# Statistics sums shared between VectorE and TensorE, and one-hots in fp8 with block sums added by VectorE, in a four-layer graph network

## The chip, the cores and the metric

The kernel runs on one core of one Trainium2 chip. The metric is the device time of one execution in microseconds (us); lower is better. TensorE is written PE, VectorE DVE, ScalarE ACT, GpSimd POOL and SyncE SP, as in the profile.

## What is computed

6250 nodes with 64 features each and 200000 edges (source, destination, 32 edge features) go through four residual layers. Cut to the parts that the change touches:

```python
z = concatenate([h[src], h[dst], e], axis=1)
gate = sigmoid(bn(z @ W_int + b_int)); upd = softplus(bn(z @ W_upd + b_upd))   # bn: mean and variance over all edges
agg = segment_sum(gate * upd, dst)                                            # layer 0
...
for l in range(3):                                                            # layer 2
    mask = clip(sigmoid(att(x[src], x[dst])) * 1.5 - 0.45, 0, 1)
    rowsum = segment_sum(mask, src) + 1e-6
    d = clip(rowsum ** -0.5, 0, 10)
    x = segment_sum((mask * d[src] * d[dst])[:, None] * x[dst], src)
    out = out + x
```

Layer 1 is a mean over neighbours and layer 3 an MLP message sum by destination.

## The kernel before, in words

The nodes stand in 49 blocks of 128. A first part of the program (count, place) sorts the edges twice, by the block of the source and by the block of the destination, into 288 steps of 7 tiles of 128 edges; all edges of one step belong to one block. Gathers from and sums into a block are then matmuls with one-hot matrices: for each tile a 128x128 matrix with a 1 where edge and node of the block meet. One-hots of the source order lie in DRAM as `hot_s`, their transposes as `turned_s`; `hot_d` and `turned_d` are those of the destination order. Before, `hot_s` and `hot_d` are bf16 (224 KB a step) and the turned ones fp8 (112 KB a step). `table_s` and `table_d` name the block of every step; the helper `Blocks.of` (L115 on) reads four of its entries into registers of the engine that asks, at the first of four steps, and `block_of` makes the address of a block from such a register.

Each stage is written by hand as one loop for each engine, with semaphores between them; a wait holds its engine's whole instruction stream, in order. The stages come one after the other, with a barrier between them. `each4` and `each12` unroll a loop by 4 or 12 steps, for buffers that are 4 or 12 deep. These stages are touched:

- `stage_conv_spread` (cs, 288 steps). DVE makes the one-hots by source (L1176) and splits the edge features; PE turns both (L1253, L1255) and forms the products (L1268 to L1271) into `cs_u_ps`; ACT casts and copies the turned ones (L1213, L1219, L1220) and a part of the result. SP stores `hot_s`, `turned_s` and `e_turned` and loads `cs_rec` (L1134) four steps ahead; POOL scatters the rows.
- `stage_conv_stats` (ct, 288 steps). DVE does four things with 896 columns in each step: the one-hot by destination of step it + 2 (L1339), the value v (L1354), the sum of the squares of the step before (L1346), and the sum of v (L1360). ACT squares v (L1386), and stages and casts the rest. PE turns the one-hot (L1402) and multiplies (L1414). SP stores `hot_d` and `turned_d`, and loads `ct_u` for step it + 4 (L1308), once ACT has squared step it.
- `stage_masks` (mask, once for each of three layers, 288 steps in 72 quads of 4). PE makes a row part for each step (L2014), ACT copies it into `mask_cols` (L1968), POOL adds the gathered columns onto it by an indirect DMA (L1956), and DVE multiplies by the attention vector (L2047) and reduces (L2052). After the fourth step of a quad, DVE `weigh`s the quad before: five instructions on 28 columns and more (L2037 to L2039, then `split3` at L806 to L809), each of which waits for the one before it. Then PE `collect`s (L2002): 28 matmuls of 3 columns that add the mask by one-hot into one PSUM bank `mask_sums_ps` for all 49 blocks, at an address from `Blocks`. SP loads `turned_s` and `hot_s` a quad at a time. At the end the bank is copied to `rowsum` (L2058).
- `stage_hop` (hop, three times, 288 steps). POOL gathers `hop_x` (L2104); ACT weights six of the seven tiles (L2120) and DVE the seventh (L2134); DVE splits them into three bf16 parts (L2143, then L2149); PE adds them by one-hot into seven PSUM banks `hop_sums_ps` for all blocks (L2167), at an address from `Blocks`. SP loads the one-hots by source, 12 steps ahead (L2085). At the end `add_zeros` closes the banks and DVE copies 3136 columns (L2153).

`stage_conv_messages` (cm) isn't changed, but it already does what the change brings to others: its sums go to two small PSUM areas, and DVE adds each to its block of `acc` (L1615), with `Blocks` on DVE:

```python
def collect(it, i, s):
    blocks = table.of(it, i)
    dve.wait_ge(summed, it + 3)
    dve.wait_ge(added, it + 2)
    s.wait()
    dve.sem_inc(gate, 1)
    to = block_of(acc, blocks[0])
    nc.vector.tensor_tensor(to, to, sums[i % 2][:, 0, :], ALU.add).then_inc(added, 1)
```

## Time and profile before

| what | value |
|---|---|
| runs | 12580.16 us median of 3 (12571.6 to 12588.71) |
| profiled execution | 12564.72 us, its span 12563.0 us |
| busy, share of the span | PE 63%, PE weight loads 59%, DVE 65%, ACT 55%, POOL 41% |
| mean granted clock of PE | 0.779 |
| cs | 2459 to 3438 us |
| ct | 3467 to 4625 us |
| mask, three times | 6869 to 7468, 8550 to 9151, 10230 to 10829 us |
| hop, three times | 7757 to 8215, 9438 to 9896, 11117 to 11577 us |

The time of the profiled execution lies 1.7 us above its span. An instruction's duration runs from its start to its end; instructions of one engine overlap, so the distance of two starts says what one costs the engine when nothing is waited for. "Idle before" is time in which the engine did nothing ahead of an instruction, and behind the arrow stands what ended it. "DVEq" and "SPq" are the sequencers of DVE and SP: register loads and the issue of DMAs.

### The profile page before, as it was taken

To read this page: it belongs to the slowest core of one execution; us is meant where nothing else is said; L and a number is where in the kernel's file an instruction comes from. 1 tells how busy PE (TensorE), PEld (TensorE's weight loads), DVE (VectorE), ACT (ScalarE), POOL (GpSimd) and SP (SyncE) were. 2 spreads that over 40 slices of the span, in tenths; PEclk is the share of its full clock that TensorE was granted. 3 is DMA by queue.
4 is the path that set the end of the run, shared out by engine and by line. 5 is a ranking of instruction groups with operands and counts; after the bars stand their busy time and mean duration, and the time that the engine had idled before them with its cause. 6 is when DMAs were issued, how large, how long until landed. Compare 5 with 4: busy or idle time off the path is not lost. (4 is left out here: it accounts for less than half of the span.)

```text
span 12563.0 us, 438885 instructions
## 1 busy us (share of the span) xinstructions
PE 7912.2 (63%) x149095; PEld 7405.0 (59%) x149106; DVE 8207.7 (65%) x17786; ACT 6913.4 (55%) x17614; POOL 5175.5 (41%) x4482
## 2 busy tenths in 40 slices
PE   6444444488855549995766656666666666565765
PEld 6333333488745448885656656565665566565765
DVE  6777777588799999981750762925718527358047
ACT  1222222299855559986217448965479764587530
POOL 2777777444300001110630752706707338345044
PEclk8555555599978879998979669787697787787997
DMA  5555543299967759987949999979999799997997
GB/s 205 166 171 167 169 140 84 83 348 348 326 195 202 201 173 319 323 275 264 346 127 349 288 262 354 297 263 300 284 324 316 226 329 290 290 335 231 366 361 226
DMA packets 1430365, 3241.49 MB, mean 258 GB/s; under 512 B 392074, under 2 KB 973252, under 8 KB 1419042
## 3 DMA queue, kind: packets, MB, share of 16 engines
q1 hardware_dynamic: 1054798, 2289.98, 52.1%
q0 software_dynamic: 331264, 823.09, 24.7%
q10 hardware_dynamic: 44116, 125.96, 3.3%
q8 instruction: 113, 1.85, 0.1%
q14 instruction: 74, 0.61, 0.0%
HBM read 2042.53 MB, written 1129.76 MB: 253 GB/s over the span
## 5 line engine op out<-in xcount | busy, mean ns | idle before, releaser
L1956 POOL DMA_INDIRECT mask_cols<-cols_all,mask_index x864 | 1372.1, 1588 | 1339.1 <-ACT mask_index L1965 1172.0
L521 POOL DMA_INDIRECT rows_s<-place_rec,place_index x1568 | 1631.1, 1040 | 538.1 <-issue 528.7
L596 PE MATMUL place_slot_ps<-place_runs,place_oh_turned 50*128 50x100 f32 x3136 | 725.8, 423 | 1231.6 <-DVE place_runs L635 1213.6
L2104 POOL DMA_INDIRECT hop_x<-cols_all,hop_index x864 | 981.2, 1136 | 1237.4 <-ACT hop_index L2111 920.0
L596 PEld LDWEIGHTS place_slot_ps<-place_runs,place_oh_turned 50*128 50x128 f32 x3136 | 683.0, 327 | 1265.9 <-issue 1265.6
L2120 ACT ACTIVATE hop_parts<-hop_x,mask 128x64 f32<-128x64 f32 x5184 | 1265.4, 334 | 47.6 <-DMA hop_x<-cols_all,hop_index 28.1
L2047 DVE SCALAR_TENSOR_TENSOR mask_hidden<-mask_cols,att 128x448 f32<-128x448 f32 x864 | 538.5, 623 | 1085.5 <-DMA mask_cols<-cols_all,mask_index 1028.8
L2167 PE MATMUL hop_sums_ps<-hop_parts,hop_onehot 128*128 128x64 bf16 x18144 | 876.0, 216 | 472.3 <-DVE hop_parts L2149 398.2
L2167 PEld LDWEIGHTS hop_sums_ps<-hop_parts,hop_onehot 128*128 128x128 bf16 x18144 | 777.0, 113 | 573.6 <-issue 572.7
L1478 POOL DMA_DIRECT2D cm_onehot<-hot_d x288 | 152.1, 528 | 2031.1 <-POOLq L104 1229.9
L2014 PE MATMUL mask_part_ps<-mask_now,mask_turned 128*128 128x64 bf16 x18144 | 912.5, 231 | 37.4 <-issue 20.9
L1968 ACT COPY mask_cols<-mask_part_ps 128x448 f32<-128x448 f32 x864 | 460.5, 533 | 841.2 <-PE mask_part_ps L2014 829.9
L550 ACT COPY place_pair_now<-place_pair 128x8 f32 x196 | 38.7, 197 | 1599.0 <-issue 1585.6
L2014 PEld LDWEIGHTS mask_part_ps<-mask_now,mask_turned 128*128 128x128 fp8e4 x18144 | 888.9, 124 | 42.9 <-issue 42.7
L2134 DVE TENSOR_TENSOR hop_parts<-hop_x,mask 128x64 f32<-128x64 f32 x864 | 189.6, 219 | 863.7 <-DMA hop_x<-cols_all,hop_index 845.0
L1687 PE MATMUL hop_in_rows_ps<-hop_in_now,hop_in_turned 128*128 128x64 bf16 x18144 | 571.7, 194 | 279.9 <-DMA hop_in_turned<-turned_d 134.0
L1687 PE MATMUL att_in_rows_ps<-att_in_now,att_in_turned 128*128 128x64 bf16 x18144 | 574.0, 194 | 253.3 <-DMA att_in_turned<-turned_d 115.6
L1687 PEld LDWEIGHTS hop_in_rows_ps<-hop_in_now,hop_in_turned 128*128 128x128 fp8e4 x18144 | 552.5, 99 | 299.4 <-issue 299.3
L1687 PEld LDWEIGHTS att_in_rows_ps<-att_in_now,att_in_turned 128*128 128x128 fp8e4 x18144 | 555.1, 99 | 272.5 <-issue 272.5
L1159 POOL DMA_INDIRECT rows_all<-cs_u,cs_index x288 | 393.9, 1368 | 639.1 <-DVE cs_u L1196 637.8
L2052 DVE TENSOR_REDUCE mask_logit<-mask_hidden 128x7 f32<-128x448 f32 x864 | 536.1, 621 | 131.2 <-DVE mask_hidden L2047 11.7
L2002 PE MATMUL mask_sums_ps<-mask_mask,mask_onehot 128*128 128x3 bf16 x6048 | 192.2, 166 | 669.5 <-DVE mask_mask L809 358.6
(392 smaller groups left out, 26453.3 us busy)
## 6 DMA issues: line engine op xcount, KB each, us to landing
cols_all<-att_in_rows SPq DMA_DIRECT2D x216, 896.0 KB
mask_onehot<-hot_s SPq DMA_DIRECT2D x216, 896.0 KB
cols_all<-hop_in_rows SPq DMA_DIRECT2D x216, 896.0 KB
hop_onehot<-hot_s SPq DMA_DIRECT2D x864, 224.0 KB
rows_all<-blank SPq DMA_DIRECT2D x72, 1808.0 KB
ct_u<-rows_all SPq DMA_DIRECT2D x288, 452.0 KB
cm_v<-rows_all SPq DMA_DIRECT2D x288, 448.0 KB
cm_onehot<-hot_d POOLq DMA_DIRECT2D x288, 448.0 KB
```

The costliest lines, as they stand in the source:

```text
L521: nc.gpsimd.indirect_dma_start(m.rows_s.rearrange("p n w -> (p n) w"), bass.IndirectOffsetOnAxis(index[:, j, t:t + 1], 0), rec[:, j, t, :] ...
L596: last = nc.tensor.matmul(slot_ps[b][:, t, 0:2 * NBK], oh_turned[:, b, t, :], runs[:, b, t, :], start=True, stop=True)
L1159: nc.gpsimd.indirect_dma_start(rows_d, bass.IndirectOffsetOnAxis(index[:, i, :], 0), u[:, i, :], None).then_inc(scattered[i], 16)
L1687: last = nc.tensor.matmul(rows_ps[i][:, t, :], turned[:, s, i, t, :], now[:, i, n, :], start=n == 0, stop=n == 2)
L1956: nc.gpsimd.indirect_dma_start(cols[:, n, :], None, table, bass.IndirectOffsetOnAxis(index[:, n, :], 0), compute_op=ALU.add).then_inc(arri ...
L1968: nc.scalar.copy(cols[:, n, :], part_ps[n % 4].rearrange("p c f -> p (c f)")).then_inc(laid, 1)
L2014: last = nc.tensor.matmul(part_ps[i][:, t, :], turned[:, s, i, t, :], now[:, i, n, :], start=n == 0, stop=n == 2)
L2047: nc.vector.scalar_tensor_tensor(out=hidden[:, j, :, :], in0=cols[:, s * 4 + i, :].rearrange("p (c f) -> p c f", f=F), scalar=0.0, in1=b2( ...
L2052: nc.vector.tensor_reduce(logit[:, s, i * BATCH:(i + 1) * BATCH], hidden[:, j, :, :], AX.X, ALU.add).then_inc(logits, 1)
L2104: nc.gpsimd.indirect_dma_start(x[:, n, :, :].rearrange("p c f -> p (c f)"), None, table, bass.IndirectOffsetOnAxis(index[:, n:n + 1], 0)). ...
L2120: last = nc.scalar.activation(parts[:, i, 0, t * F:(t + 1) * F], x[:, s * 4 + i, t, :], ACT.Copy, scale=mask[:, bass.ds(it * BATCH + t, 1)])
L2167: last = nc.tensor.matmul(block_of(sums, blocks[0]), onehot[:, s, i, t, :], upper(parts[:, i, q, t * F:(t + 1) * F]), start=False, stop=False)
```

## The change

There are two parts. In ct the sum of v is divided: DVE adds four of the seven tiles (512 columns), and PE adds the other three (384 columns) with one f32 matmul of the identity a step into a PSUM bank that is copied out at the end. For source-ordered one-hots, cs makes them in fp8, `hot_s` in DRAM is half as wide, and mask and hop load them so; in both of these stages each block sum goes to a small PSUM area of its own, and DVE adds it to its block in SBUF. PE no longer reads the block table there; DVE does.

```diff
 def stage_conv_spread
-        onehot = sb("onehot", [P, 4, BATCH, P], bf16)
+        onehot = sb("onehot", [P, 4, BATCH, P], fp8)
...
-                                            ALU.is_equal).then_inc(hot, 1)
+                                            ALU.is_equal, saturate=False).then_inc(hot, 1)
 def stage_conv_stats
+        totaled = sem("totaled")
+        OWN = 4
+        total_ps = ctx.enter_context(nc.psum_tensor("ct_total_ps", [P, 512], fp32))[:, 0:(BATCH - OWN) * W].rearrange("p (c w) -> p c w", w=W)
...
                     dve.wait_ge(squared, it + 1)
+                    dve.wait_ge(totaled, it + 1)
...
-                    nc.vector.tensor_tensor(sum_acc[:], sum_acc[:], v[:, i % 2, :, :], ALU.add).then_inc(summed, 1)
+                    nc.vector.tensor_tensor(sum_acc[:, 0:OWN, :], sum_acc[:, 0:OWN, :], v[:, i % 2, 0:OWN, :], ALU.add).then_inc(summed, 1)
...
+                dve.wait_ge(totaled, IT + 3)
+                nc.vector.tensor_copy(sum_acc[:, OWN:BATCH, :], total_ps)
...
                     last.then_inc(spread, 1)
+                    if not isinstance(it, int) or it > 0:
+                        add_up(it - 1, (i - 1) % 2)
+
+                def add_up(it, j):
+                    pe.wait_ge(valued, it + 3)
+                    pe.sem_inc(gate, 1)
+                    nc.tensor.matmul(total_ps.rearrange("p c w -> p (c w)"), m.ident[:], v[:, j, OWN:BATCH, :].rearrange("p c w -> p (c w)"),
+                                     start=False, stop=False).then_inc(totaled, 1)
 def stage_masks
-        onehot = sb("onehot", [P, 3, 4, BATCH, P], bf16)
+        onehot = sb("onehot", [P, 3, 4, BATCH, P], fp8)
...
-        sums = ctx.enter_context(nc.psum_tensor(f"{name}_sums_ps", [P, 512], fp32))[:, 0:3 * NB].rearrange("p (b c) -> p b c", c=3)
+        sums = [ctx.enter_context(nc.psum_tensor(f"{name}_sums_ps{j}", [P, 512], fp32))[:, 0:12].rearrange("p (h c) -> p h c", c=3)
+                for j in range(3)]
+        added = sem("added")
...
                     pe.wait_ge(masked, quad + 1)
+                    pe.wait_ge(added, quad * 4 + 4)
                     pe.sem_inc(gate, 1)
                     for h in range(4):
-                        blocks = quads.of(quad * 4 + h, h)
                         for t in range(BATCH):
-                            last = nc.tensor.matmul(block_of(sums, blocks[0]), onehot[:, s, h, t, :], mask3[:, s, h * BATCH + t, :],
-                                                    start=False, stop=False)
+                            last = nc.tensor.matmul(sums[s][:, h, :], onehot[:, s, h, t, :], mask3[:, s, h * BATCH + t, :],
+                                                    start=t == 0, stop=t == BATCH - 1)
...
+                def add_rows(quad, s):
+                    dve.wait_ge(summed, quad + 1)
+                    for h in range(4):
+                        blocks = quads.of(quad * 4 + h, h)
+                        dve.wait_ge(added, quad * 4 + 12 + h)
+                        dve.sem_inc(gate, 1)
+                        to = block_of(rowsum, blocks[0])
+                        nc.vector.tensor_tensor(to, to, sums[s][:, h, :], ALU.add).then_inc(added, 1)
...
                         weigh(k * 3 + s - 1, (s - 1) % 3, k, order)
+                    if i == 3 and (not isinstance(it, int) or it > 18):
+                        add_rows(k * 3 + s - 4, (s - 1) % 3)
...
-                dve.wait_ge(summed, QUADS + 1)
-                nc.vector.tensor_copy(rowsum, sums)
+                for quad in range(QUADS - 4, QUADS):
+                    add_rows(quad, quad % 3)
 def stage_hop
-        onehot = sb("onehot", [P, 3, 4, BATCH, P], bf16)
+        onehot = sb("onehot", [P, 3, 4, BATCH, P], fp8)
...
-        sums = ctx.enter_context(nc.psum_tensor(f"{name}_sums_ps", [P, 56, F], fp32))
+        sums = [ctx.enter_context(nc.psum_tensor(f"{name}_sums_ps{j}", [P, 512], fp32))[:, 0:F] for j in range(4)]
+        added = sem("added")
...
                     nc.vector.tensor_tensor(last, rest, upper(rest), ALU.subtract).then_inc(parted, 1)
+                    if not isinstance(it, int) or it > 1:
+                        collect(it - 2, (i - 2) % 4)
+
+                def collect(it, i):
+                    blocks = table_s.of(it, i)
+                    dve.wait_ge(summed, it + 5)
+                    dve.wait_ge(added, it + 4)
+                    dve.sem_inc(gate, 1)
+                    to = block_of(acc, blocks[0])
+                    nc.vector.tensor_tensor(to, to, sums[i], ALU.add).then_inc(added, 1)
+                nc.vector.memset(acc, 0.0).then_inc(added, 1)
...
-                dve.wait_ge(summed, IT + 5)
-                nc.vector.tensor_copy(acc, sums[:, 0:NB, :])
...
-                    blocks = blocks_s.of(it, i)
+                    pe.wait_ge(added, it + 1)
...
-                add_zeros(nc, m, sums[:], False).then_inc(summed, 1)
 def build
-        m.hot_s, m.hot_d = (dram(n, [P, NBT, C * P // 2]) for n in ("hot_s", "hot_d"))
+        m.hot_s, m.hot_d = dram("hot_s", [P, NBT, C * P // 4]), dram("hot_d", [P, NBT, C * P // 2])
```

## Rows read from the trace of the kernel before

**Rows 1.** Windows, one a stage (cs, ct, first mask, first hop): stretch, length, busy time by engine, clock, DMA share, GB/s.

```profile
2459.00:3438.00 979.00, 838.09 (x14112) 796.54 (x14112) 806.35 (x2304) 872.66 (x1440) 393.92 (x288) 0.99 0.97 343
3467.00:4625.00 1158.00, 630.62 (x8065) 577.16 (x8065) 1153.88 (x1153) 645.62 (x1148) 0.00 (x0) 0.81 0.72 200
...
6869.00:7468.00 599.00, 366.63 (x8066) 355.70 (x8066) 442.32 (x1081) 274.25 (x938) 456.33 (x288) 0.67 1.06 276
...
7757.00:8215.00 458.00, 293.23 (x6060) 257.02 (x6062) 403.33 (x866) 422.88 (x1800) 327.40 (x288) 0.76 0.92 289
```

**Rows 2.** Timeline of ct: start, duration, engine, line, operation.

```profile
4001.20 1.21 DVE L1354 TENSOR_TENSOR ct_v<-ct_v_ps,ct_u 128x896 f32<-128x896 f32 x1
...
4003.84 0.35 SPq L1308 DMA_DIRECT2D ct_u<-rows_all  x1
...
4004.20 1.21 DVE L1339 TENSOR_TENSOR ct_onehot<-iota_p,ct_u 128x896 bf16<-128x896 f32 x1
```

**Rows 3.** Timeline of DVE in cm.

```profile
5001.38 0.39 DVE L1615 TENSOR_TENSOR acc<-acc,cm_sums_ps 128x64 f32 x1
5001.51 1.26 DVE L1591 TENSOR_TENSOR cm_v<-cm_v_ps,cm_v 128x896 f32<-128x896 f32 x1
```

**Rows 4.** Groups by line, PE: busy, mean ns | idle before, releasers.

```profile
L1402 PE MATMUL ct_turn_ps<-ident_b,ct_onehot 128*128 128x128 bf16 x2016 | 186.9, 242 | 553.2 <-DVE ct_onehot L1339 553.2
...
L940 PE MATMUL att_hid<-turned_l,w_att 65*128 65x448 f32 x84 | 44.7, 671 | 5.5 <-PEq L104 5.5
```

**Rows 5.** Timeline at the start of ct.

```profile
3462.37 1.78 SPq L1308 DMA_DIRECT2D ct_u<-rows_all  x4
...
3466.27 3.32 DVE L1339 TENSOR_TENSOR ct_onehot<-iota_p,ct_u 128x896 bf16<-128x896 f32 x3 [0.49 <-DMA ct_u<-rows_all]
```

**Rows 6.** Groups by line, ACT in cs.

```profile
L1213 ACT COPY cs_e<-cs_rec 128x448 f32<-128x448 f32 x288 | 162.7, 565 | 73.7 <-PE cs_e_ps L1255 37.8 <-DMA cs_rec<-rows_s 30.3
```

**Rows 7.** DMA of the mask stage, 6900 to 7400 us: SP's queue, packets, MB, share.

```profile
q1 hardware_dynamic: 17854, 85.34, 43.7%
```

**Rows 8.** Timeline of DVE in the first mask stage, around two quads' ends.

```profile
7107.64 0.21 DVE L809 TENSOR_TENSOR mask_mask<-mask_mask_now,mask_mask 128x28 bf16<-128x28 f32 x1
7108.36 0.63 DVE L2047 SCALAR_TENSOR_TENSOR mask_hidden<-mask_cols,att 128x448 f32<-128x448 f32 x1 [0.51 <-issue]
...
7113.37 0.62 DVE L2047 SCALAR_TENSOR_TENSOR mask_hidden<-mask_cols,att 128x448 f32<-128x448 f32 x1
...
7114.67 0.17 DVE L2037 TENSOR_SCALAR mask_mask_now<-mask_logit 128x28 f32<-128x28 f32 x1
7114.87 0.18 DVE L2038 TENSOR_SCALAR mask_mask_now<-mask_mask_now 128x28 f32<-128x28 f32 x1
7115.21 0.20 DVE L2039 COPY mask<-mask_mask_now 128x28 f32 x1 [0.16 <-DVE mask_mask_now L2038]
7115.30 0.19 DVE L806 CAST mask_mask<-mask_mask_now 128x28 bf16<-128x28 f32 x1
...
7116.19 0.62 DVE L2047 SCALAR_TENSOR_TENSOR mask_hidden<-mask_cols,att 128x448 f32<-128x448 f32 x1
```

**Rows 9.** One line's instructions, L2047 in the first mask stage: durations, first and last start.

```profile
L2047 DVE SCALAR_TENSOR_TENSOR mask_hidden<-mask_cols,att x288: 614/625/667, 6885.2 to 7461.0; 128x448 f32<-128x448 f32 x144
```

**Rows 10.** Waits in the first mask stage, 6900 to 7440 us: total, times, longest.

```profile
DVE mask_hidden L2047 <- DMA mask_cols<-cols_all,mask_index: 46.7, 89, 1.5
```

**Rows 11.** One line's instructions (L121, L1615) in cm: duration ns min/median/max.

```profile
L121 DVEq TENSOR_LOAD <-table_d x72: 340/344/607, 4708.3 to 5619.6; - x72
...
L1615 DVE TENSOR_TENSOR acc<-acc,cm_sums_ps x288: 214/386/417, 4710.2 to 5630.6; 128x64 f32 x144
```

**Rows 12.** Timeline of DVE in the first hop stage.

```profile
7902.17 0.63 DVE L2143 TENSOR_TENSOR hop_parts<-hop_parts 128x448 f32<-128x448 f32 x1
...
7902.94 0.62 DVE L2149 TENSOR_TENSOR hop_parts<-hop_parts 128x448 f32<-128x448 f32 x1
7903.60 0.62 DVE L2143 TENSOR_TENSOR hop_parts<-hop_parts 128x448 f32<-128x448 f32 x1
```

More of the change, by code:

```diff
@@ L1991, in _ @@
             def _(pe):
-                quads = Blocks(nc, pe, m.table_s)
-                add_zeros(nc, m, sums, True)
                 def collect(quad, s, k):
@@ L2028, in _ @@
                 dve.sem_inc(logits, 2)
+                dve.sem_inc(added, 11)
+                quads = Blocks(nc, dve, m.table_s)
+                nc.vector.memset(rowsum, 0.0).then_inc(added, 1)
+                def add_rows(quad, s):
[6 more added lines that the diff above has]
+                        nc.vector.tensor_tensor(to, to, sums[s][:, h, :], ALU.add).then_inc(added, 1)
                 def weigh(quad, s, k, order):
@@ L2149, in step @@
                     nc.vector.tensor_tensor(last, rest, upper(rest), ALU.subtract).then_inc(parted, 1)
+                    if not isinstance(it, int) or it > 1:
[7 more added lines that the diff above has]
+                    nc.vector.tensor_tensor(to, to, sums[i], ALU.add).then_inc(added, 1)
+                table_s = Blocks(nc, dve, m.table_s)
+                dve.sem_inc(added, 3)
+                nc.vector.memset(acc, 0.0).then_inc(added, 1)
                 scale_seventh(0, 0, 0)
-                each12(dve, step)
-                dve.wait_ge(summed, IT + 5)
-                nc.vector.tensor_copy(acc, sums[:, 0:NB, :])
+                each12(dve, step, first=2)
+                collect(IT - 2, (IT - 2) % 4)
+                collect(IT - 1, (IT - 1) % 4)
             @block.tensor
             def _(pe):
-                blocks_s = Blocks(nc, pe, m.table_s)
-                add_zeros(nc, m, sums[:], True)
                 def step(it, s, i, k, more, _):
@@ L2166, in step @@
                         for q in range(3):
-                            last = nc.tensor.matmul(block_of(sums, blocks[0]), onehot[:, s, i, t, :],
-                                                    upper(parts[:, i, q, t * F:(t + 1) * F]), start=False, stop=False)
+                            last = nc.tensor.matmul(sums[i], onehot[:, s, i, t, :],
+                                                    upper(parts[:, i, q, t * F:(t + 1) * F]),
+                                                    start=t == 0 and q == 0, stop=t == BATCH - 1 and q == 2)
                     last.then_inc(summed, 1)
                 each12(pe, step)
-                add_zeros(nc, m, sums[:], False).then_inc(summed, 1)
 def build(nc, a, out):
```

7 lines of the change are left out of this document (5 added, 2 removed).

## The prediction, written before the changed kernel ran

> **What bounds the kernel now.** The stages follow one another, so the change is priced stage by stage, and the first view is that of the windows [rows 1]. In ct DVE is busy 1154 of 1158 us: nothing else sets that time. In cs no engine is full (PE 838, ACT 873 of 979 us), while the DMA engines are busy 0.97 of it. In mask no engine is full either (DVE 442, POOL 456 of 599 us) and the DMA share is 1.06, so the DMAs seem to bound it; but a busy share hides short waits between dependent instructions, so the timeline must say how much room DVE has. In hop ACT leads with 423 of 458 us, DVE with 403 is close behind, DMA 0.92.
>
> **Statistics (ct).** DVE starts an 896-column instruction each 1.00 us: from L1354 at 4001.20 to L1339 at 4004.20 are three [rows 2], so a step is 4.00 us. In cm a sum of 64 columns takes 0.13 between starts [rows 3]; so a column costs (1.00 - 0.13) / 832 = 1.05 ns, and 512 columns 0.60 us. DVE alone would go at 3.60: 288 x 0.40 = 115 us less. PE gets an f32 matmul of 384 columns; 448 columns took 671 ns [rows 4], so about 0.6 us and a weight load. PE waits 553 us / 288 = 1.92 us a step for the one-hot just there [rows 4], so that is hidden; without this cover it would be 288 x 0.6 = 170 us. What is late next is the load of `ct_u`. It is issued 2.64 us after the start of v (4003.84 against 4001.20 [rows 2]), since SP waits for the square, and serves the one-hot of step it + 4, which DVE starts 1.00 us before v of step it + 4 - 2, two steps on. The first load of the stage took 3.90 us from its issue to the start of the one-hot, which waited for it [rows 5]. So with a step of P, 2P - 1.00 is at least 2.64 + 3.90, and P at least 3.77 us. At 4.00 there are 0.46 us to spare over the two steps, and no wait; at 3.60 there would be. I take 3.78: 288 x 0.22 = **-63 us**; bounds 0 (the load gets slower as it is asked for more often) and -115 (later loads faster than the first).
>
> By the Trainium skill (DMA: Bandwidth & Descriptors, Anatomy of one DMA) a DMA costs about 2.0 us fixed and its bytes / 436e3: for 452 KB about 3.1 us, an estimate by that page, under which ct would give the whole -115. The 3.90 us of [rows 5] speak against it.
>
> **One-hots in fp8, cs.** DVE, PE and ACT issue what they did. SP's store of `hot_s` falls from 224 to 112 KB a step: 33 MB of 343 GB/s x 979 us = 336 MB [rows 1], a tenth. If the DMAs alone bound cs that would be 98 us. But ACT is at 873 of 979, and only part of its idle time ends with a DMA: 30 us at L1213 [rows 6]. I take these and a third more for the like on DVE: **-40 us**; bounds 0 and -98.
>
> **Masks.** Removed: half the one-hot load. 60 quads in 500 us by 896 KB are 55 of the 85 MB of SP's queue with its share of 0.437 [rows 7]; half of that is 0.14 of DMA time. Also removed: PE's table reads, its closing zero matmul and the copy of `rowsum`, all small beside the rest. Added on DVE for each quad: `add_rows`. What is DVE's room? A step without waits is L2047 to L2037, 7113.37 to 7114.67 = 1.30 us; `weigh` is 7114.67 to 7116.19 = 1.52; where the loop branches, one quad in three, the way from L809 to L2047 is 0.72 (7107.64 to 7108.36); I take 0.5 of it as extra [rows 8]. A quad is 4 x 1.30 + 1.52 + 0.17 = 6.89 us, 72 quads 496. DVE's part of the stage goes from 6885.2 [rows 9] to the end at 7468 [rows 1], 583 us, so it waits about 87; 46.7 us of 540 stand as waits for the gathers [rows 10]. DVE is thus 85% filled by dependent work and not, as the busy time says, 74%.
>
> The price of `add_rows`: first the table is read into registers, 0.344 us [rows 11]; with the register work, the wait and the address I take 0.83 from the last instruction of `weigh` to the first add. Then each of the three further adds waits for the one before it, by `added`, and takes its address from a register. Its nearest row is L2038 to L2039: 0.34 us between starts, 0.18 of it duration and 0.16 wait and address [rows 8]; the mark on `gate` is an instruction of its own here, for which I add 0.1. So 0.44 each. The way back to L2047 costs 0.1. Sum 0.83 + 3 x 0.44 + 0.1 = 2.25 us a quad, 162 a stage. Bounds: 1.1 (four adds at 0.20, the table read not much more than its 0.344) and 3.0 (each add at the 0.386 of L1615 [rows 11] and 0.26 around it). The new quad is 9.1 us; POOL's 456 us for 288 gathers are 1.58 each, with the pause of about 0.3 behind each 7.5 us a quad, and don't bind; neither do the DMAs with less to move. Of the waits some 8 us of start and 3 of end are left: 496 + 162 + 11 = 669 against 583, +86 a stage, **+258 us**. PE's `collect` now waits for `added` too, and behind it stand the row parts of the next quad; but DVE needs these two quads (18 us) later, so it costs nothing while POOL has under 9.1 us of work a quad.
>
> Here the Trainium skill speaks against my price (VectorE: DVE Perf Modes, The DRAIN you can't avoid): the next operation doesn't start before the pipeline is empty, with or without a semaphore, so a semaphore costs nothing extra. The trace disagrees: L806 follows L2039, on which it doesn't wait, after 0.09 us, and L2038 follows L2037, on which it does, after 0.20 [rows 8].
>
> **Hops.** A step is 1.43 us on DVE (7902.17 to 7903.60) [rows 12], paced by ACT. DVE's own need is 0.77 from L2143 to L2149 and 0.53 for the 448 columns of L2149 (0.66 are taken): 1.30. The add of 64 PSUM columns costs 0.13 between starts, as in cm [rows 3]: 1.43, a tie with ACT. One step in four also reads the table. In cm long instructions queued ahead cover that; here DVE's sequencer has only L2149's 0.53 us ahead of it for table, waits and address, by the 0.83 above and the wait of the next L2143 about 0.45 us too little: +0.11 a step, and branches +0.04. 288 x 0.15 = 43 us, of which I take 27 as absorbed by waits that the stage has today (458 us against 288 x 1.43 = 412), and which the halved one-hot load shrinks. The closing copy of 3136 columns (3.3 us at 1.05 ns) and the zero matmuls go, about 5 us; the memset of `acc` lies beside the first gather. Net +11 a stage, **+35 us**; bounds -60 (all open time hidden, fewer waits) and +150 (0.17 us a step more).
>
> **The sum.** -63 - 40 + 258 + 35 = +190 us, on the profiled execution's 12565 (span 12563): 12755. The median stands 15 us above that execution, and the forecast is for a median: rounded within those 15, **12760**. My forecast's own range is 12640 to 12860.
>
> **The rivals.** (1) *Waits on DVE's own work are nearly free or hidden*: `add_rows` costs 0.35 for the table and 4 x 0.2 for the adds, 1.15 us a quad, 83 a stage, which the 87 us of waits take up. Then masks +3 each, ct -63, cs -40, hops 0: about 12475, faster. It decides where the price is under 1.1 us a quad. For it: cm, where such adds cost 0.13 [rows 3]. Against: [rows 8]. 0.10. The rule of The DRAIN you can't avoid in the Trainium skill would lead here. (2) *Halved DMAs pay everywhere*: cs -90, ct -115, hops -20 each, masks as forecast: 12565 + 258 - 265 = 12558, no change. For it: DMA shares of 0.92 and more [rows 1]. Against: [rows 5, 6]. 0.10. (3) *Hops become DVE's too*: 0.17 us a step more than ACT's pace, +50 a stage: 12870. For it: the tie at 1.43 [rows 12]. 0.14. That the change doesn't do what it says gets nothing: the adds and waits are in the code.
>
> **The numbers.** Forecast 0.66, rivals 0.10, 0.10 and 0.14. The range leaves out rival 1 and part of 2: 12600 to 12890. About 0.2% (25 us) is what a measurement of this kernel can tell from no change. Faster: 0.10 and 0.03 of rival 2, 0.13; same 0.05; slower 0.82.
>
> **What would show it.** In the changed profile: ct steps of 3.78 us with DVE waiting for `ct_u` before L1339 (3.60 and no wait would be rival 2's part); masks of about 685 us with the starts of the adds 0.44 apart, and few waits for gathers left; cs near 940; hops near 470 with a gap at every fourth add. I am wrong if a mask stage stays at 600 us or under.

## The result: slower by 1.3%, by the predicted sum

The changed kernel takes **12743.42 us** (median of 4 runs, 12737.16 to 12750.6), the kernel before 12584.43 us (4 runs, 12571.6 to 12589.0): a ratio of **1.0128**, 95% interval 1.0113 to 1.0143. Predicted were 12760 us and a range of 12600 to 12890. The profiled execution took 12750.6 us with a span of 12749.0, 186 us more than the 12563.0 of the kernel before; the prediction's sum was +190.

By stage, from the first to the last instruction that writes one of the stage's own tiles, in us. The last adds of a mask stage, and the closing copy of a hop in the kernel before, write tensors that outlive the stage, and so fall into the pause behind:

| stage | before | changed | difference | predicted |
|---|---|---|---|---|
| spread (cs) | 977.8 | 934.9 | -43 | -40 |
| statistics (ct) | 1159.9 | 1109.1 | -51 | -63 |
| three masks | 597.2, 599.8, 597.4 | 671.7, 673.8, 674.2 | +225 | +258 |
| pause behind each mask | 15.9, 16.4, 15.9 | 20.1, 20.8, 20.2 | +13 | in the +258 |
| three hops | 453.5, 453.5, 455.4 | 466.3, 468.3, 465.4 | +38 | } |
| pause behind each hop | 68.5, 65.9, 72.0 | 63.5, 63.9, 67.0 | -12 | } +35 |
| placement, not touched | 2135.7 | 2142.7 | +7 | 0 |

These make +177 of the +186; the rest lies in untouched stages, no one of which moved by over 6 us. The +13 behind the masks come of the last fourteen adds, which run behind TensorE's last sum; counted to the last add, the mask stages grew by 79, 78 and 81 us. Of the -12 behind the hops some 10 are the closing copies of 3.4 us each, which are gone.

The first view is again that of the windows, one a stage, of the changed kernel (stretch and its length; then busy time of PE, PEld, DVE, ACT, POOL; TensorE's granted clock, DMA share, GB/s), to be held against [rows 1]:

```profile
2463.90:3398.80 934.90, 836.34 (x14112) 794.64 (x14112) 787.58 (x2304) 866.06 (x1440) 308.76 (x287) 0.99 0.94 323
3426.60:4535.60 1109.00, 704.37 (x8642) 533.96 (x8642) 1059.03 (x1155) 647.88 (x1152) 0.00 (x0) 0.99 0.76 210
6787.20:7458.90 671.70, 367.16 (x8064) 358.15 (x8064) 477.40 (x1359) 270.33 (x938) 450.17 (x288) 0.66 0.93 197
7754.80:8221.20 466.40, 319.57 (x6048) 286.38 (x6048) 428.43 (x1152) 430.79 (x1800) 295.74 (x288) 0.66 0.82 213
```

VectorE's busy time in the mask stage grew by 35 us only (442 to 477) while the stage grew by 75, and every engine and the DMA queues are less full than before (DMA 1.06 to 0.93). A stage that gets slower while each of its resources gets emptier waits for a chain, and only the timeline shows it. VectorE at the end of a quad of the changed kernel (start, duration, engine, line, operation, the idle time before it):

```profile
7105.73 0.21 DVE L809 TENSOR_TENSOR mask_mask<-mask_mask_now,mask_mask 128x28 bf16<-128x28 f32 x1
7106.53 0.16 DVE L2056 TENSOR_TENSOR rowsum<-rowsum,mask_sums_ps 128x3 f32 x1 [0.60 <-issue]
7106.94 0.16 DVE L2056 TENSOR_TENSOR rowsum<-rowsum,mask_sums_ps 128x3 f32 x1 [0.25 <-DVE rowsum L2056]
7107.33 0.16 DVE L2056 TENSOR_TENSOR rowsum<-rowsum,mask_sums_ps 128x3 f32 x1 [0.24 <-DVE rowsum L2056]
7107.73 0.16 DVE L2056 TENSOR_TENSOR rowsum<-rowsum,mask_sums_ps 128x3 f32 x1 [0.24 <-DVE rowsum L2056]
7108.43 0.63 DVE L2075 SCALAR_TENSOR_TENSOR mask_hidden<-mask_cols,att 128x448 f32<-128x448 f32 x1 [0.54 <-issue]
```

The first add starts 0.80 us behind L809, the others 0.41, 0.39 and 0.40 apart: four instructions with 0.64 us of work. This is a quad at whose end the loop branches: from the start of L809 to the start of the next step were 0.72 us in [rows 8], and are now 2.70, so 1.98 more. At the two ends of three where the loop doesn't branch it is 2.06 and 1.98. 72 quads at about that are some 143 us, and the waits that the stage had before take up nearly half of it.

In the statistics the step is bound by the load, as said. Timeline of two steps of the changed kernel:

```profile
4001.27 0.35 SPq L1311 DMA_DIRECT2D ct_u<-rows_all  x1
...
4002.52 1.08 DVE L1359 TENSOR_TENSOR ct_v<-ct_v_ps,ct_u 128x896 f32<-128x896 f32 x1
...
4004.40 0.86 PE L1430 MATMUL ct_total_ps<-ct_v,ident 128*128 128x384 f32 x2
4004.52 0.68 DVE L1365 TENSOR_TENSOR sum_acc<-sum_acc,ct_v 128x512 f32<-128x512 f32 x1
4005.03 0.35 SPq L1311 DMA_DIRECT2D ct_u<-rows_all  x1
4005.38 1.09 DVE L1343 TENSOR_TENSOR ct_onehot<-iota_p,ct_u 128x896 bf16<-128x896 f32 x1 [0.18 <-DMA ct_u<-rows_all]
4006.39 1.08 DVE L1359 TENSOR_TENSOR ct_v<-ct_v_ps,ct_u 128x896 f32<-128x896 f32 x1
```

The load of 4001.27 serves the one-hot of 4005.38, two steps on, which waits for it: 4.11 us from issue to use, where the first load of the stage had taken 3.90 [rows 5]. The next load is issued 2.51 us behind the start of v (4005.03 against 4002.52), 2.64 in [rows 2]. The prediction's relation with these, (2.51 + 4.11 + 1.01) / 2, gives a step of 3.82; from v to v it is 3.87 here. PE's sum of 384 columns runs as two matmuls, 0.86 us in all, beside VectorE's work, and nobody waits for it. And the clock that TensorE was granted in ct is 0.99, the 2.4 GHz level, against 0.81 [rows 1]; TensorE was busy 704 of 1109 us where it had been 631 of 1158. No time hangs on it, since VectorE waits for the load and not for TensorE.

In the hops one step in four stands out, the one with the table read:

```profile
7902.46 0.65 DVE L2180 TENSOR_TENSOR hop_parts<-hop_parts 128x448 f32<-128x448 f32 x1
7903.27 0.22 DVE L2190 TENSOR_TENSOR H<-H,hop_sums_ps 128x64 f32 x1 [0.16 <-PE hop_sums_ps L2208]
7903.44 0.62 DVE L2174 TENSOR_TENSOR hop_parts<-hop_parts 128x448 f32<-128x448 f32 x1
...
7904.22 0.62 DVE L2180 TENSOR_TENSOR hop_parts<-hop_parts 128x448 f32<-128x448 f32 x1
7904.76 0.21 DVE L2190 TENSOR_TENSOR H<-H,hop_sums_ps 128x64 f32 x1
```

From L2180 to the add are 0.81 us with the read and 0.54 without. The profile names TensorE as releaser, but this comes every fourth step.

### The profile page after: what moved, and what is told of

It is laid out like the page before. It is cut to its first block and busy times, and to the rows that moved or that the text cites. A ratio compares the mean times of both kernels' runs of the same rounds, so it can differ in the third digit from the quotient of the medians.

```text
span 12749.0 us, 445377 instructions
## 1 busy us (share of the span) xinstructions
PE 8080.8 (63%) x149631; PEld 7469.2 (59%) x149636; DVE 8275.9 (65%) x19515; ACT 6919.2 (54%) x17614; POOL 4991.2 (39%) x4482
## 5 line engine op out<-in xcount | busy, mean ns | idle before, releaser
L2135 POOL DMA_INDIRECT hop_x<-cols_all,hop_index x864 | 894.0, 1035 | 1404.2 <-ACT hop_index L2142 945.1
L2208 PE MATMUL hop_sums_ps<-hop_parts,hop_onehot 128*128 128x64 bf16 x18144 | 963.8, 224 | 453.0 <-DVE H L2190 269.9
L2208 PEld LDWEIGHTS hop_sums_ps<-hop_parts,hop_onehot 128*128 128x128 fp8e4 x18144 | 863.5, 118 | 553.2 <-issue 552.9
L2019 PEld LDWEIGHTS mask_sums_ps<-mask_mask,mask_onehot 128*128 128x128 fp8e4 x6048 | 179.3, 104 | 915.6 <-issue 915.5
L1271 PE MATMUL cs_u_ps<-cs_now,cs_turned 128*128 128x128 bf16 x6048 | 578.5, 219 | 0.0
## 6 DMA issues: line engine op xcount, KB each, us to landing
ct_u<-rows_all SPq DMA_DIRECT2D x288, 452.0 KB
```

The source lines that it names most:

```text
L1271: last = nc.tensor.matmul(at, turned[:, i, t, :], now[:, i, n, :], start=False, stop=n == 2)
L2135: nc.gpsimd.indirect_dma_start(x[:, n, :, :].rearrange("p c f -> p (c f)"), None, table, bass.IndirectOffsetOnAxis(index[:, n:n + 1], 0)). ...
L2208: last = nc.tensor.matmul(sums[i], onehot[:, s, i, t, :], upper(parts[:, i, q, t * F:(t + 1) * F]), start=t == 0 and q == 0, stop=t == BAT ...
```

## The experiments

The theory after the result had four claims: the mask loss is the serial chain of four adds at a place where VectorE has nothing else queued; the statistics' gain is cut by the ring of load, add, square, load; the hops pay for the table read; and the parts add up, since they lie in different stages. The rivals are named in the expectations. The runs came from different chips, and each group was timed beside the kernel before: a first group (12557.72 us median of the kernel before, 6 runs), a second (12553.97, 7 runs), a third on a chip on which it took 13321.95 (7 runs), and a last one (12562.89, 7 runs). Ratios are to the kernel before of the same group; stage times are to the last write of a stage tile, as above. Where an edit moves adds into or out of the pause behind a mask stage, stage and pause together are given too (613, 616 and 613 us in the kernel before, 692, 695 and 694 in the changed one).

### One part alone: the statistics

The kernel before with the changed statistics stage (its matmul onto `total_ps` with it) and nothing else.

```diff
- nc.vector.tensor_tensor(sum_acc[:], sum_acc[:], v[:, i % 2, :, :], ALU.add).then_inc(summed, 1)
+ nc.vector.tensor_tensor(sum_acc[:, 0:OWN, :], sum_acc[:, 0:OWN, :], v[:, i % 2, 0:OWN, :], ALU.add).then_inc(summed, 1)
```

> The kernel before with the statistics part alone. Theory (the parts add up, and ct is paced by the load of ct_u): ct goes from 1160 to about 1109 us as in the changed kernel, step 3.82 us, cs, masks and hops stay as before; total 50 us below the kernel before, 0.4%. Rival (in the changed kernel ct is slowed by something of the other part): ct below 1080 us here.

Measured: 12503.66 us, ratio 0.9959 (0.9939 to 0.9978). The stage takes 1103.1 us, 57 less; spread (976.7), masks (597.8, 595.1, 596.2) and hops (456.6, 456.9, 456.0) stay within 5 us of the table above. The group of the one-hots in it:

```profile
L1343 DVE TENSOR_TENSOR ct_onehot<-iota_p,ct_u 128x896 bf16<-128x896 f32 x263 | 286.8, 1090 | 35.4 <-DMA ct_u<-rows_all 27.8 <-issue 1.1
```

The wait for the load is there without any other part of the change, so the fp8 one-hots and the block sums have no share in it.

### One part alone: the block sums on VectorE, one-hots in bf16

Against the changed kernel (the statistics as before, too):

```diff
- onehot = sb("onehot", [P, 3, 4, BATCH, P], fp8)
+ onehot = sb("onehot", [P, 3, 4, BATCH, P], bf16)
```

> The kernel before with the block sums on VectorE in masks and hops alone, one-hots still bf16. Theory (VectorE's chain of add_rows paces the masks, the DMAs don't): each mask stage about 672 us, as in the changed kernel, although 112 KB a step more are loaded; cs unchanged at 978; hops 466 to 480 us, by the waits for the larger one-hots; total 240 to 290 us above the kernel before. Rival (masks are bound by the DMAs): masks above 700 us.

Measured: 12865.86 us, ratio 1.0246 (1.0216 to 1.0275). Masks 672.9, 675.5 and 680.1, hops 473.3, 474.3 and 478.0, spread 977.4. The total, 308 us over the kernel before, lies above the 240 to 290 that were expected, though each stage came as expected. The block sums alone cost the masks all that they cost in the changed kernel, and the smaller one-hots are worth at most 6 us a mask stage there. In the spread, which the sums don't touch, the 42 us from 977 to 935 come with the smaller one-hots: the two others of this group, with fp8, have 937 and 938, both with bf16 have 977 (976.7 and 977.4). The reverse, fp8 one-hots with PE's block sums as before, was not tried.

### The wait between the adds

The changed kernel with four accumulators, one for each add of a quad, summed once at the end:

```diff
- dve.wait_ge(added, quad * 4 + 12 + h)
+ if h == 0:
+     dve.wait_ge(added, quad * 4 + 12)
- to = block_of(rowsum, blocks[0])
+ to = block_of(four[:, h, :, :], blocks[0])
```

> The changed kernel with four accumulators in each mask stage, one for each of the four adds of a quad, so that an add never waits for the add before it; the four are summed once at the end of the stage (two instructions). Same number of adds. Theory (the price is the wait for VectorE's own result, 0.2 us of the 0.40 between the adds): the adds start 0.2 us apart, a mask stage falls by 72 x 3 x 0.2 = 43 us, to about 630. Rival (a wait on one's own engine costs nothing extra, the adds cost 0.4 us by themselves): masks stay at 672.

Measured: 12623.95 us, ratio 1.0052 (1.0029 to 1.0075); masks 642.1, 643.0 and 642.1, 30 to 32 less each, and about 35 less with the pauses. Its timeline at a quad's end:

```profile
7108.19 0.21 DVE L809 TENSOR_TENSOR mask_mask<-mask_mask_now,mask_mask 128x28 bf16<-128x28 f32 x1
7108.98 0.87 DVE L2058 TENSOR_TENSOR mask_four<-mask_four,mask_sums_ps 128x3 f32 x4 [0.59 <-issue]
7110.42 0.62 DVE L2077 SCALAR_TENSOR_TENSOR mask_hidden<-mask_cols,att 128x448 f32<-128x448 f32 x1 [0.57 <-issue]
```

Four adds of 0.16 us take 0.87 from the first start to the last end: (0.87 - 0.16) / 3 = 0.237 between starts, where it was 0.40. So the wait for the add before makes 0.16 us of each gap, less than the 0.2 that was expected; the rest is the add's own duration and 0.08 more. 3 x 0.16 x 72 quads are 35 us, which is what came back with the pauses. The 0.16 is the price at this place and not of every wait for an own result: in `weigh` five of the seven instructions wait so too (all but L2037 and L806), and in [rows 8] L2038 starts 0.20 behind L2037. The one at 0.34, L2039, takes an address from a register, as the adds do; whether that makes the difference no run tried. The first add still starts 0.79 behind L809: that is the table read, which this edit leaves.

### The place of the adds

The changed kernel with one add in each step, between the product and the reduction, in place of four in a row at every fourth step. Each of these adds waits for the one before it, and the table is read once a quad, as before.

```diff
+ if not isinstance(it, int) or it > 15:
+     add_row(k * 3 + s - 4, (s - 1) % 3, i)
  dve.wait_ge(hid, it + 13)
...
- if i == 3 and (not isinstance(it, int) or it > 18):
-     add_rows(k * 3 + s - 4, (s - 1) % 3)
```

> The changed kernel with the four adds of a quad put one into each step, between L2047 and the reduce that waits for it, where VectorE idles 0.24 us today. Same adds, same waits, same table read. Theory (the adds are dear only because nothing lies between them): they cost nearly nothing there but for the table read (under 0.5 us a quad); a mask stage falls to 540 to 580 us, where GpSimd's gathers (7.5 us a quad) bind. Rival (four adds cost the same wherever they stand): 672 us. Between them, about 620, the sequencer's own time counts.

Measured: **12414.44 us, ratio 0.9886 (0.9857 to 0.9915)**, faster than both kernels. Masks 568.4, 569.2 and 569.2: 104 less than in the changed kernel and 29 less than in the kernel before; with the pause behind, 24 to 26 less than before.

```profile
7106.28 0.62 DVE L2075 SCALAR_TENSOR_TENSOR mask_hidden<-mask_cols,att 128x448 f32<-128x448 f32 x1
7107.45 0.16 DVE L2056 TENSOR_TENSOR rowsum<-rowsum,mask_sums_ps 128x3 f32 x1 [0.55 <-PE mask_sums_ps L2019]
7107.67 0.62 DVE L2082 TENSOR_REDUCE mask_logit<-mask_hidden 128x7 f32<-128x448 f32 x1
7108.21 0.61 DVE L2075 SCALAR_TENSOR_TENSOR mask_hidden<-mask_cols,att 128x448 f32<-128x448 f32 x1
7108.74 0.15 DVE L2056 TENSOR_TENSOR rowsum<-rowsum,mask_sums_ps 128x3 f32 x1
7108.97 0.62 DVE L2082 TENSOR_REDUCE mask_logit<-mask_hidden 128x7 f32<-128x448 f32 x1
7109.51 0.61 DVE L2075 SCALAR_TENSOR_TENSOR mask_hidden<-mask_cols,att 128x448 f32<-128x448 f32 x1
```

Look at the step of 7108.21: with an add in it, it is 1.30 us long, exactly the 1.30 of [rows 8] without one. The reduction waits for the product in front of it anyway; the add fits into that wait, starts 0.53 behind the product, and its own wait for the add before has been over for a step. Only the step with the table read is longer, 1.93 (7106.28 to 7108.21). The profile names TensorE there, but by the code the sums that this add takes were done two quads earlier.

### What binds the masks once the adds are free

The changed kernel with the adds of the row sums and TensorE's wait for them left out.

```diff
- pe.wait_ge(added, quad * 4 + 4)
...
- if i == 3 and (not isinstance(it, int) or it > 18):
-     add_rows(k * 3 + s - 4, (s - 1) % 3)
```

> The changed kernel with the adds of the row sums in the three mask stages left out, and TensorE's wait for them with them (the row sums stay zero, so this part of the computation is missing); one-hots, block sums of TensorE and all traffic stay. In the profile of the changed kernel a mask stage takes 672 to 674 us; with one add in each step it takes 569. Theory (the adds cost only because VectorE paces the stage; without them the next limit is near 560, which is where the spread adds have come to already): 545 to 575 a stage, the kernel near 12400. Rival (the gain of the spread adds came from elsewhere and VectorE still paces the stage at 569): 500 to 540 a stage without the adds. Second rival (transfers pace the stage): not under 600.

Measured: 12409.13 us, ratio 0.9882 (0.9862 to 0.9901); masks 570.6, 571.5 and 566.5. Without any add the stages are as long as with one a step; with the pause behind, where the last adds stand, they are 2 to 7 us shorter. So spread adds cost next to nothing. The windows 6900 to 7300 us, first of this kernel, then of the one with spread adds:

```profile
6900.00:7300.00 400.00, 255.23 (x5776) 248.40 (x5774) 311.42 (x777) 195.73 (x670) 336.59 (x209) 0.68 1.05 237
```

```profile
6900.00:7300.00 400.00, 262.32 (x5891) 255.52 (x5892) 329.69 (x1002) 199.17 (x682) 335.71 (x212) 0.68 1.06 240
```

VectorE is busy 311 of 400 us without the adds and 330 with them, and the stage doesn't care: it isn't VectorE's any more. GpSimd's own row of the waits of the kernel without adds:

```profile
POOL mask_cols L1976 <- issue: 37.8, 124, 0.3
...
POOL mask_cols L1976 <- ACT mask_cols L1988: 14.6, 48, 0.3
POOL mask_cols L1976 <- ACT mask_index L1985: 11.3, 37, 0.3
```

336.6 us of gathers and 63.7 of pauses between them fill the 400. All 209 pauses are about 0.3 us, whatever the profile names as their end, so GpSimd goes from gather to gather without a longer wait. It paces the stage, at 400 / 209 = 1.91 us a gather, 7.7 a quad. In the changed kernel the same engine waited 87.5 us of the 400 for the indices, which is what an engine does that runs at another's pace, VectorE's.

### The load of the statistics

The changed kernel; SyncE's load waits for the copy of the map (L1392 there), the slot's last reader, and no longer for the square behind it:

```diff
- sp.wait_ge(squared, it + 3)
+ sp.wait_ge(mapped, it + 1)
...
- nc.scalar.copy(m.map_d[:, bass.ds(it, 1)], u[:, i, C * W + C:UW])
+ nc.scalar.copy(m.map_d[:, bass.ds(it, 1)], u[:, i, C * W + C:UW]).then_inc(mapped, 1)
```

> The changed kernel with one edit in the statistics stage: SyncE's load of the rows of step i+4 (the 452 KB that fill ct_u) waits for ScalarE's copy of the map, the last reader of that slot, and no longer for the square behind it. In the profile of the changed kernel the stage takes 1109 us in 290 steps (3.82 each) and VectorE's one-hots wait 38 us for this load. Theory (the ring of load, add, square, load paces the stage and keeps back what the removed columns gave): the load starts about 1 us earlier, the step falls to about 3.6 and the stage to 1040 to 1070, the kernel by 40 to 70 us, to about 12690. Rival (the DMA queues' own throughput, or TensorE's f32 sum of 384 columns in a step, paces it): the stage stays within 10 us of 1109.

Measured: 12662.84 us, ratio 1.0084 (1.0063 to 1.0104), against the 1.0128 of the changed kernel; the stage takes 1045.6 us, 63.5 less than in the changed kernel and 114 less than in the kernel before. The groups by line from 3500 to 4400 us:

```profile
L1344 DVE TENSOR_TENSOR ct_onehot<-iota_p,ct_u 128x896 bf16<-128x896 f32 x250 | 270.3, 1081 | 0.0
...
L1431 PE MATMUL ct_total_ps<-ct_v,ident 128*128 128x384 f32 x500 | 216.1, 514 | 0.0
```

and the window of nearly the whole stage:

```profile
3430.00:4450.00 1020.00, 685.04 (x8465) 520.23 (x8465) 1016.34 (x1128) 633.23 (x1126) 0.00 (x0) 1.00 0.81 223
```

250 steps in 900 us are 3.60 each, the step that the prediction worked out for VectorE alone. The wait for the load is gone, VectorE is busy 1016 of 1020 us, and the DMA queues carry 223 GB/s where they had carried 210. So it was the ring and not the queues.

### The table read of the hops

The changed kernel; VectorE's sequencer reads the table behind L2174, where it waits for other engines, and the add takes the values:

```diff
  nc.vector.tensor_tensor(rest, whole, upper(whole), ALU.subtract).then_inc(halved, 1)
+ if not isinstance(it, int) or it > 1:
+     table_s.of(it - 2, (i - 2) % 4)
...
- blocks = table_s.of(it, i)
+ blocks = table_s.values[i:i + 1]
```

> The changed kernel with one edit in the hops: VectorE's sequencer reads the step's block number from its table right behind the one-hots of the step, where it waits about 0.5 us for other engines anyway, and no longer between two pieces of VectorE work. Theory (in the hops the change costs VectorE's own path, the table read of about 0.34 us and the one wait more): each hop falls from 466 to 450 or so, 40 us in all, with 10 to 60 as the range. Rival (the hop is paced by the gathered rows or by TensorE, and the read lies in idle time already): each hop stays within 5 us of 466.

Measured: 12697.64 us, ratio 1.0111 (1.0091 to 1.0132), too near the 1.0128 of the changed kernel to say much by itself. The stages say more: hops 452.3, 453.0 and 452.2, 13 to 15 less each. Its timeline:

```profile
7902.66 0.62 DVE L2174 TENSOR_TENSOR hop_parts<-hop_parts 128x448 f32<-128x448 f32 x1
...
7904.10 0.62 DVE L2174 TENSOR_TENSOR hop_parts<-hop_parts 128x448 f32<-128x448 f32 x1
...
7908.44 0.61 DVE L2174 TENSOR_TENSOR hop_parts<-hop_parts 128x448 f32<-128x448 f32 x1
```

Four steps from 7902.66 to 7908.44 are 5.78 us, 1.44 or 1.45 each and none longer than its neighbours by the 0.3 us of before.

### The three edits together

Spread adds, early load and early table read in one kernel (the diffs are those above).

> The changed kernel with three edits together: in the masks one add in each step in place of four in every fourth (12414 us when it ran alone), the early load of the statistics, and the early table read of the hops. If the three gains lie in different stages and add up: 12414 - 50 (statistics) - 40 (hops) = about 12325, with 12280 to 12400 as the range. If neither the load nor the table read is on the path of its stage: 12400 to 12420.

Measured: **12310.07 us (4 runs, 12302.39 to 12316.14), ratio 0.9804 (0.9788 to 0.9821)**. Masks 569.8, 568.4 and 567.6, statistics 1045.9, hops 452.0, 450.1 and 452.4: each stage has what its edit gave alone.

### One size: four tiles on TensorE

```diff
- OWN = 4
+ OWN = 3
```

> The kernel with the three edits (12310 us) and one size changed: TensorE sums four of the seven tiles (512 columns) in the statistics, VectorE three (384). With the early load VectorE is busy 1016 of 1020 us there, so it is the bound. Theory (VectorE's step of 3.60 us loses 128 columns at about 1.1 ns each, 0.13 to 0.14 us): the stage falls from 1046 by 35 to 40 us to about 1008, the kernel to about 12272. Rival (the next limit is within that: the rows' load, a ring of 3.5 to 3.6 us, or the DMA queues at 0.81 of their time): the stage falls by under 15 us. Second rival (TensorE's f32 sum grows to be late for VectorE's next write of the same tile): the stage grows.

Measured on the slower chip: 13074.24 us, ratio 0.9818 (0.9802 to 0.9834). The statistics take 1014.5 us, 31 less than 1045.9; masks 567.9, 567.9 and 567.6. Hops are 527 to 530, not 450 to 452 as on the other chip. The ratio could not say whether the total had gained, so the kernel ran once more:

> The kernel with the three edits and four tiles on TensorE once more: its first runs came from a chip on which the kernel before took 13322 us instead of 12554, with the extra time in the stages that are paced by gathered or small transfers, and the statistics at 1014.5 us (1046 with three tiles). If that chip alone hides the gain in the total: on a chip where the kernel before takes 12550 to 12590, this takes 12270 to 12310 (12310 less 31), a ratio of 0.977 to 0.979. If the fourth tile gives the time back elsewhere: 12305 to 12340, a ratio of 0.980 or more. On a chip like the last one: 13070 to 13080 again, which tells nothing new.

Measured: **12290.12 us (4 runs, 12287.42 to 12291.0), ratio 0.9785 (0.9769 to 0.9802)**, the fastest of the study and 2.15% under the kernel before; the statistics take 1015.0 us. From 12310.07 that is 20 us in the medians, across two chips whose kernels before differ by 9 us, and 31 us in the stage. In the two profiled executions the span fell by 15, and the pause behind the placement, which no edit touches, was 10 us longer (125.9 against 115.6). The wait for the load begins to come back, which may be where the 4 to 9 us short of the expected 35 to 40 went (groups by line, 3500 to 4400 us):

```profile
L1344 DVE TENSOR_TENSOR ct_onehot<-iota_p,ct_u 128x896 bf16<-128x896 f32 x258 | 279.9, 1085 | 3.2 <-DMA ct_u<-rows_all 1.4 <-issue 0.2
```

258 steps in 900 us are 3.49 each.

### The smaller one-hots, taken back

Two kernels on the slower chip: the changed one and the one with the three edits, both with one-hots by source in bf16 (fill, store and load).

```diff
- m.hot_s, m.hot_d = dram("hot_s", [P, NBT, C * P // 4]), dram("hot_d", [P, NBT, C * P // 2])
+ m.hot_s, m.hot_d = (dram(n, [P, NBT, C * P // 2]) for n in ("hot_s", "hot_d"))
...
- onehot = sb("onehot", [P, 3, 4, BATCH, P], fp8)
+ onehot = sb("onehot", [P, 3, 4, BATCH, P], bf16)
```

> The changed kernel with the one-hots by source kept, stored and loaded in bf16 again; the statistics' sum on TensorE and VectorE's block sums stay. Worked out from the runs so far: the block sums with bf16 one-hots were 308 us over the kernel before and the statistics alone 54 below it, which would put the two together at 12812; the changed kernel is 12743, so the one-byte one-hots would be worth about 70 us, from spread (935 against 977 us), the hops (466 against 473 to 478) and the masks (673 against 676). Theory (the parts lie in different stages and add up): 12790 to 12830, spread at 977, hops at 474, masks at 673 to 680. Rival (part of the spread's gain is the statistics stage's or run to run): under 12780.

Measured: 13521.19 us, ratio 1.0153 (1.0132 to 1.0173). The total can't be held against the changed kernel's: on this chip the placement stage, which no kernel here touches, took 2433.8 us against 2142.7. Spread 983.1, statistics 1099.5, masks 672.9, 678.1 and 675.0, hops 534.7, 538.7 and 539.2. The theory's total, 12790 to 12830, was thus not tested; its masks of 673 to 680 were met.

> The kernel with the three edits (12310 us) with one-hots by source in bf16 again. In it the masks take 569 us and GpSimd is busy 336 of 400 us there with gathers, at a DMA share of 1.06; in the kernel before, with bf16 one-hots, the share was 1.09 and the gathers waited more. Theory (the smaller one-hots are worth little in the masks, 3 to 10 us each, 42 in the spread and 8 to 15 in each hop): 70 to 110 us over 12310, so 12380 to 12420, still under the kernel before. Rival (with the adds spread the transfers of bf16 one-hots become the bound of the masks): 590 or more a mask stage, the kernel over 12430.

Measured: 13208.63 us, ratio 0.9918 (0.9898 to 0.9938). On the same chip the fp8 kernel with four tiles took 13074.24, which is 134 us less; 31 of them are the statistics' fourth tile, which leaves about 103. The differences of spread, masks and hops alone add up to 120, and untouched stages and pauses came out some 15 shorter. So the theory's sum (70 to 110) is met by the total and missed by the stages, and its parts did not hold: masks 603.2, 596.0 and 595.0 against 568, 27 to 35 each and not 3 to 10; hops 6 to 9 each; the spread 985.2 against 981.3, 4 and not 42. The rival is the one that came true in the masks. Windows of 400 us in the first mask stage, first bf16, then fp8, and the kernel before:

```profile
7250.00:7650.00 400.00, 259.22 (x5613) 253.00 (x5614) 327.41 (x956) 189.59 (x651) 320.95 (x202) 0.64 1.09 288
```

```profile
7250.00:7650.00 400.00, 262.24 (x5883) 254.72 (x5881) 331.81 (x1003) 195.05 (x688) 335.67 (x212) 0.69 1.05 241
```

```profile
6900.00:7300.00 400.00, 255.14 (x5600) 247.90 (x5600) 307.55 (x753) 189.30 (x650) 319.77 (x203) 0.67 1.09 286
```

Same mask code, same chip, one-hots of twice the size: 288 against 241 GB/s, 202 gathers against 212. The first line and that of the kernel before are nearly one: a DMA share of 1.09, 288 and 286 GB/s, 202 and 203 gathers. The masks took 597 to 600 there with all the adds on TensorE, and 595 to 603 here with all the adds on VectorE. That larger one-hots make this stage longer once the adds are spread is shown by the change of size. That the same limit held the kernel before at 597 is argued from the likeness of the two windows; fp8 one-hots with the adds on TensorE would show it and were not tried. The waits say a part of the way. GpSimd's for ScalarE's copies of the indices (total, times, longest), bf16, then fp8:

```profile
POOL mask_cols L1977 <- ACT mask_index L1986: 26.2, 29, 1.9
```

```profile
POOL mask_cols L1977 <- ACT mask_index L1986: 6.7, 22, 0.3
```

With fp8 no pause of GpSimd is over 0.3 us; with bf16 some last up to 1.9, and their 20 us more are about the ten gathers that are missing. By the code, ScalarE copies an index once VectorE has made the product of twelve steps before. What holds VectorE there isn't shown: neither kernel's VectorE waits over 5 us of the 400 for gathers.

## Why the prediction was right, step by step

**Masks.** The mechanism and the price held. Of the 2.25 us a quad, the 0.83 to the first add measured 0.80, and the 0.44 between adds 0.40. Where the loop branches that makes 1.98 us a quad, as above. 162 us of adds were to take up most of the 87 us of waits and to come out at +86; measured +79 to the last add. The four-accumulator run shows the wait's part of the price, the kernel without adds (103 us less a stage) that nothing but the adds held the stage there. Over three stages the term was too large by 20 us. Two larger errors nearly cancel in it. The adds of a quad cost 2.02 us on average over the stage and not 2.25, 17 us a stage less. But the quad without adds and waits is 7.10 and not 6.89, 15 us a stage more: `weigh` takes 1.47 us from L2065 to L809 on average (1.42 in the kernel before), where the one quad of [rows 8] has 1.30. So the forecast quad of 9.1 us was met by the measured mean of 9.16 in part by luck, and the room for the adds was 72 us rather than 87.

The rule of the Trainium skill (VectorE: DVE Perf Modes, The DRAIN you can't avoid), under which a semaphore between two operations costs nothing extra, is contradicted for these adds by two runs that differ in this wait: 0.40 us between the starts of the same adds with it and 0.237 without (the runs differ in the accumulators too, which the adds address in the same way). Rival 1, which rested on that, stood at 12475. Rival 2 would have had 90 us in the spread and 115 in the statistics, where 43 and 51 came. The spread adds show what rival 1 had in mind, and more: when the price is hidden, the stage drops below the time of the kernel before, to its next limit.

**One thing in this step was wrong.** The prediction took the 87 us of waits as room that the adds could fill and held them to be the DMAs' doing, with GpSimd's 7.5 us a quad far off. Two limits stand near each other instead. At 568 us it is GpSimd, at 7.7 to 7.9 us a quad, as the kernel without adds shows. At about 597 it is the transfers of bf16 one-hots: measured with spread adds, and argued for the kernel before. The halved one-hots took the second away, and the adds in one lump hid this: 676 against 673. Had the price been free, the masks would have come out 24 to 30 us *under* the kernel before, and rival 1's +3 each was mis-sized by that.

**Statistics.** The bound by the ring was right, and its terms too: issue 2.51 behind v (2.64 taken), 4.11 from issue to use (3.90 taken), a step of 3.82 (3.78 taken) and -51 for -63. The term that was too small is the load's own time. The early-load run shows that the ring was the cause: without it the stage gives 114 us, the 115 that the prediction had for VectorE alone. PE's sum was sized too small, at 0.6 us for 0.86, and nothing waited for it. The Trainium skill's cost of a DMA (DMA: Bandwidth & Descriptors, Anatomy of one DMA), about 3.1 us for these 452 KB as an estimate, would have given -115; the section fits it to DMAs that GpSimd issues, and this load is SyncE's. The load took 4.11 and the stage gave 51.

**Spread.** -43 for -40. In the first group and against the kernel before the stage is about 40 us shorter with the fp8 one-hots; on the slower chip it is 4. The same instructions ran on both, so this points to the transfers, as the prediction had it, but no run separates them. The 40 itself was a choice (the waits of one line and a third more), so meeting it to 3 us is luck.

**Hops.** +38 in the stages and -12 behind them make +26 for the +35 taken. The step with the table is 0.3 us longer than the others, where 0.45 was priced; the early-table run takes 14 us a stage away, which is all that the hop stages had lost. Rival 3 needed 0.17 us a step and did not come.

## To carry to other kernels

An add that costs 0.16 us is free or costs 0.5, by where it stands: put small dependent operations one by one into waits that the engine has anyway, never in a row at a place where its queue is empty, and read registers ahead of time. When a ring of load and use paces a stage, look at which reader the load waits for, since the last one that truly reads the slot is often earlier than the one it waits for. And a part that frees a resource can look worthless (6 us) beside a part that makes another one the bound; judged with that one mended it was worth 30.

## What the runs showed of the hardware that was not expected

- The f32 matmul of 384 columns stands as two instructions a step (x500 in 250 steps, 514 ns each by the profile), and with 512 columns still as two; together 0.86 us for 384. The 671 ns of [rows 4] were already those of one of two: its 84 records are 42 matmuls (ScalarE reads their results 21 times, two at a time).
- Between adds that take their address from a register, VectorE's wait for its own last result costs 0.16 us: 0.40 against 0.237 between starts. Between two instructions of `weigh` with such a wait it is 0.20 from start to start (L2037 to L2038), against 0.09 without one (L2039 to L806) [rows 8].
- One of the chips was 6% slower. On it, the kernel before took 13321.95 us; placement took 2424 us in the kernel with four tiles against 2143 in the changed kernel, and its hops 527 against 451 in the same kernel on the other chip, while masks (568) and statistics (1014.5 against 1015.0) were the same to 1 or 2 us. Early table reads were worth 4 us at most in its hops (535.7 to 537.0 with the edit, 534.7 to 539.2 without, both in bf16). The ratio to the kernel before hid it (0.9818 against 0.9785 for the same kernel); the stage times showed it at once.
